# A fused linear-attention and quantised FFN block on one core: reciprocals first on the DMA queue, x by rows two tiles ahead, denominators in front of the products of Q with the state

## What is computed

```python
q, k, v = (norm(x) @ Wq.T + bq), (norm(x) @ Wk.T + bk), (norm(x) @ Wv.T + bv)   # 16 heads of 32
q, k = elu(q) + 1, elu(k) + 1
numerator   = einsum('bhtd,bhtde->bhte', q, cumsum(outer(k, v)))   # causal linear attention
denominator = maximum(einsum('bhtd,bhtd->bht', q, cumsum(k)), 1e-6)
x = x + norm((numerator / denominator) @ Wo.T + bo)
h = mx_quantize(norm(x))              # 32 values share a scale, values on the FP6 grid
x = x + norm(h @ mx_quantize(weight).T + bias)
```

## Time and profile before

| | us |
|---|---|
| median of three runs | 2397.83 |
| lowest and highest | 2393.44, 2398.91 |
| the profiled execution's own time | 2399.21 |
| its span, first to last instruction | 2397.4 |
| mean granted clock of TensorE | 0.993 |

### The profile page before, as it was taken

The page is one execution under the profiler, slowest core; times in us unless marked ns, Lnnn a source line. Parts: engine busy times, 40 slices in busy tenths (PEclk is TensorE's granted clock), DMA queues, the critical chain, the costliest instruction groups (busy, mean ns, idle before and its releaser), DMA issues.

```text
span 2397.4 us, 63827 instructions
## 1 busy us (share of the span) xinstructions
PE 2332.0 (97%) x26146; PEld 1905.0 (79%) x26146; DVE 1984.1 (83%) x3988; ACT 1080.8 (45%) x1840; POOL 1470.3 (61%) x1730
## 2 busy tenths in 40 slices
PE   7999999999999999999999999999999999999997
PEld 5877888888788788888787887888878888878785
DVE  7888889888788888898888887888988888878886
ACT  4444444444444444444444444444444444444442
POOL 2566566666566665666665665656666656656554
PEclk9999999999999999999999999999999999999999
DMA  4222221222222322222322222222123222223211
GB/s 158 71 92 98 75 77 62 88 99 73 86 65 75 99 90 80 77 65 86 99 73 90 73 71 91 96 76 75 62 89 99 73 90 73 71 91 95 77 46 37
DMA packets 108227, 195.55 MB, mean 82 GB/s; under 512 B 15136, under 2 KB 21664, under 8 KB 107424
## 3 DMA queue, kind: packets, MB, share of 16 engines
q1 hardware_dynamic: 107936, 191.47, 24.5%
HBM read 155.65 MB, written 35.78 MB: 80 GB/s over the span
## 4 chain that ended last, share of the span: by engine, by line
PE 79%; DMA 7%; DVE 4%; ACT 3%; issue 3%; POOL 2%; SPq 2%; POOLq 0%; DVEq 0%; ACTq 0%
PE work L423 12%; PE work L425 11%; PE work L424 11%; PE score L423 10%; PE score L424 10%; PE score L425 10%; PE work L540 5%; PE work L442 4%; PE score L505 4%; DMA rden_dram<-rinv 3%; DMA kc<-rden_dram 3%; PE state_bank L553 1%; POOL f_buf L1425 1%; DVE A L1020 1%; PE score L527 1%
## 5 line engine op out<-in xcount | busy, mean ns | idle before, releaser
L1020 DVE TENSOR_TENSOR A<-score,causal 128x512 f32<-128x512 f32 x512 | 329.2, 681 | 21.5 <-PE score L505 21.5
L1395 POOL TENSOR_TENSOR exp_t<-exp_t,x_coef 128x512 f32<-128x512 f32 x124 | 198.5, 1601 | 148.6 <-DMA exp_t<-in_xt 148.6
L725 ACT CAST oT_hi<-kc 128x512 fp32r<-128x512 f32 x128 | 79.6, 622 | 365.4 <-DVE kc L1015 365.4
L1402 POOL TENSOR_TENSOR x_res<-x_res,o_buf 128x512 f32<-128x512 f32 x128 | 175.6, 1372 | 104.5 <-ACT o_buf L670 104.5
L423 PE MATMUL work<-wo_hi,oT_hi 128*128 128x512 f32 x512 | 204.2, 399 | 14.8 <-ACT Kn L720 11.9
L423 PE MATMUL work<-wv_hi,xT_hi 128*128 128x512 f32 x512 | 214.9, 420 | 0.0
L423 PE MATMUL score<-xT_hi,wq_hi 128*128 128x512 f32 x512 | 208.1, 406 | 6.8 <-DVE KT L960 6.8
L1397 POOL TENSOR_TENSOR exp_t<-exp_t,x_coef 128x512 f32<-128x512 f32 x124 | 205.2, 1655 | 9.7
L423 PE MATMUL score<-xT_hi,wk_hi 128*128 128x512 f32 x512 | 205.7, 402 | 0.0
L425 PE MATMUL work<-wv_hi,xT_lo 128*128 128x512 f32 x512 | 202.2, 395 | 0.6 <-issue 0.6
L424 PE MATMUL work<-wv_lo,xT_hi 128*128 128x512 f32 x512 | 201.8, 394 | 0.9 <-issue 0.9
(11 more groups left out here) (134 smaller groups left out, 6393.1 us busy)
## 6 DMA issues: line engine op xcount, KB each, us to landing
x_in<-in_x SPq DMA_DIRECT2D x128, 256.0 KB, 4.3
x_res<-in_x SPq DMA_DIRECT2D x128, 256.0 KB, 2.8
kc<-rden_dram SPq DMA_DIRECT2D x128, 256.0 KB
exp_t<-in_xt SPq DMA_DIRECT2D x124, 256.0 KB, 3.1
out<-f_buf SPq DMA_DIRECT2D x96, 256.0 KB, 2.0
x_coef<-coef_dram SPq DMA_DIRECT2D x31, 512.0 KB, 3.8
out<-xd SPq DMA_DIRECT2D x32, 256.0 KB, 2.1
rden_dram<-rinv SPq DMA_DIRECT2D x32, 64.0 KB, 3.5
```

What stands on the lines that cost most here:

```text
L1020: nc.vector.tensor_tensor(A[:, j, :, :], score_bank[j][:], causal[:].unsqueeze(1).to_broadcast([P, G, P]), ALU.mult).then_inc(a_set, 1)
L1395: nc.gpsimd.tensor_tensor(rows, rows, by_token(0), ALU.mult).then_inc(x_scaled, 1)
L1402: nc.gpsimd.tensor_tensor(x_res[:, b, :], x_res[:, b, :], o_buf[:, b % 2, :], ALU.add).then_inc(r_set, 1)
```

## The change

Four things are moved; no computation is added or taken away.

- SyncE: load_x (x by rows) is issued for tile i+2 instead of i+1, spread over the turn, with tile 1's ahead of the first turn. store_rden comes ahead of the loads of x by features, and these stand between the four spreads. load_res(0) comes behind the third spread, load_res(1), (2) and (3) at the end of the turn, behind store(i-1, 3) and load_x(i+2, 3).
- TensorE: denominators ahead of past_products.
- ScalarE: among others kn(1) ahead of o_hi(0), seed(2) ahead of x_hi(1), xd_hi(1) behind k(3).
- VectorE and GpSimd: the order within the turn is written anew. f_seen(1), its join and its widen stand between phi_q(3) and product(3); x_lo(0) ahead of v_bias(1); o_lo(3) ahead of r_seen(1), as before; x_lo(3) behind quantise(0); output(2) between x_scale(0) and x_scale(1); residual(2) ahead of dequantise(1).

```diff
@@ SyncE, turn @@
-                if nxt:
-                    load_x(i + 1, 0)
-                    load_x(i + 1, 1)
-                    load_x(i + 1, 2)
-                    load_x(i + 1, 3)
+                after = i + 2 < TILES
                 if prev:
                     store(i - 1, 0)
-                if cur:
-                    load_res(i, 0)
+                if after:
+                    load_x(i + 2, 0)
+                    load_x(i + 2, 1)
                 if nxt:
                     store_coef(i + 1)
                     spread_coef(i + 1)
                 if prev:
                     store(i - 1, 1)
-                if cur:
-                    load_res(i, 1)
-                if nxt:
-                    load_xt(i + 1, 0)
-                    load_xt(i + 1, 1)
+                if after:
+                    load_x(i + 2, 2)
                 if cur:
                     store_rden(i)
                     spread_rden(i, 0)
+                if nxt:
+                    load_xt(i + 1, 0)
+                if cur:
                     spread_rden(i, 1)
-                    spread_rden(i, 2)
-                    spread_rden(i, 3)
+                if nxt:
+                    load_xt(i + 1, 1)
                 if prev:
                     store(i - 1, 2)
                 if cur:
-                    load_res(i, 2)
+                    spread_rden(i, 2)
+                    load_res(i, 0)
                 if nxt:
                     load_xt(i + 1, 2)
+                if cur:
+                    spread_rden(i, 3)
+                if nxt:
                     load_xt(i + 1, 3)
                 if prev:
                     store(i - 1, 3)
+                if after:
+                    load_x(i + 2, 3)
                 if cur:
+                    load_res(i, 1)
+                    load_res(i, 2)
                     load_res(i, 3)
@@ TensorE, turn @@
                 f(2)
                 xd_transposes(3)
+                denominators()
                 past_products()
-                denominators()
                 v(0)
@@ ScalarE, turn @@
+                kn(0)
                 seed(0)
-                kn(0)
+                kn(1)
                 o_hi(0)
-                seed(1)
                 if nxt:
                     x_hi(i + 1, 0)
                 f_norm(2)
-                kn(1)
+                seed(1)
+                seed(2)
                 if nxt:
                     x_hi(i + 1, 1)
                 o_hi(1)
                 o_norm(i, 0)
                 kn(2)
-                seed(2)
+                o_hi(2)
+                seed(3)
+                kn(3)
@@ VectorE, turn @@
                 phi_q(0)
+                phi_q(1)
                 xd_lo(2)
-                phi_q(1)
...
-                f_bias(1)
+                phi_q(2)
+                product(2)
+                phi_q(3)
                 f_seen(1)
-                phi_q(2)
...
                 join(i - 1, "f", 1)
-                phi_q(3)
-                product(2)
                 widen(i - 1, "f", 1)
                 product(3)
-                f_bias(2)
                 xd_lo(3)
-                f_seen(2)
                 clamp()
                 invert()
```

More of the change, by code:

```diff
@@ L410, in _ @@
                 load(dst[:], src.to_broadcast([P, D]), small_loaded)
+            for b in range(NSEQ):
+                load_x(1, b)
             turn(0, False, True, True)
@@ L860, in turn @@
                     x_hi(i + 1, 2)
-                o_hi(2)
-                kn(3)
-                seed(3)
                 r_norm(i, 0)
@@ L1251, in turn @@
-                xd_lo(1)
                 join(i - 1, "r", 3)
-                f_seen(0)
-                widen(i - 1, "r", 3)
-                greatest(i - 1, 2)
                 scan(2)
                 join(i - 1, "f", 0)
+                greatest(i - 1, 2)
+                widen(i - 1, "r", 3)
+                scale(i - 1, 2)
                 widen(i - 1, "f", 0)
-                scale(i - 1, 2)
+                xd_lo(1)
                 quantise(i - 1, 2)
+                phi_k(3)
                 if nxt:
-                    widen(i + 1, "x", 2)
+                    join(i + 1, "x", 2)
+                    x_seen(i + 1, 3)
@@ L1263, in turn @@
                 greatest(i - 1, 3)
                 scale(i - 1, 3)
-                phi_k(3)
+                f_bias(1)
                 scan(3)
-                quantise(i - 1, 3)
-                phi_q(0)
-                xd_lo(2)
-                phi_q(1)
                 if nxt:
                     join(i + 1, "x", 3)
-                f_bias(1)
-                f_seen(1)
-                phi_q(2)
+                    widen(i + 1, "x", 2)
+                quantise(i - 1, 3)
                 if nxt:
@@ L1289, in turn @@
+                f_seen(2)
                 v_bias(0)
                 mask(0, 0)
+                join(i - 1, "f", 2)
                 widen(i - 1, "f", 2)
@@ L1296, in turn @@
                 normalise(0)
+                mask(1, 0)
+                f_seen(3)
+                mask(1, 1)
                 o_lo(0)
-                f_seen(3)
-                mask(1, 0)
-                mask(1, 1)
-                join(i - 1, "f", 3)
+                if nxt:
+                    x_lo(i + 1, 0)
                 v_bias(1)
                 mask(1, 2)
+                join(i - 1, "f", 3)
                 mask(1, 3)
+                widen(i - 1, "f", 3)
                 o_bias(i, 0)
-                widen(i - 1, "f", 3)
                 o_seen(i, 0)
-                if nxt:
-                    x_lo(i + 1, 0)
+                normalise(1)
                 join(i, "o", 0)
                 widen(i, "o", 0)
-                normalise(1)
                 mask(2, 0)
@@ L1318, in turn @@
                 mask(2, 2)
+                v_bias(2)
                 mask(2, 3)
-                v_bias(2)
                 r_seen(i, 0)
                 o_bias(i, 1)
+                o_seen(i, 1)
                 join(i, "r", 0)
-                o_seen(i, 1)
+                widen(i, "r", 0)
                 normalise(2)
-                join(i, "o", 1)
                 mask(3, 0)
                 mask(3, 1)
-                widen(i, "r", 0)
+                mask(3, 2)
                 o_lo(2)
-                mask(3, 2)
-                if nxt:
-                    x_lo(i + 1, 2)
+                join(i, "o", 1)
                 mask(3, 3)
+                v_bias(3)
                 widen(i, "o", 1)
-                v_bias(3)
                 greatest(i, 0)
```

70 lines of the change are left out of this document (35 added, 35 removed).

## The result

The changed kernel takes **2472.07 us**, the median of four runs (2460.7 to 2478.17); the kernel before takes 2397.15 (2393.44 to 2398.91) beside it. The ratio is 1.0309, with a 95% interval from 1.0269 to 1.035. The forecast was 2427 and the range ended at 2453: the sign was right, the size was not.

A forecast was written before the change was run, and what follows sets the result against it. TensorE, busy for 97% of the span, was taken to set the time. Kn and masks -21, denominators +27, "issue" -6 and x_res +29 made +29 us; 2399.2 + 29 - 1.4 = 2427 us, range 2385 to 2453.

The forecast's parts named there:

- x_res(1): Its load at the turn's end delays residual(1) through to TensorE's transposes of xd(0): 0.95 us per tile, +29 us (0 to 40).
- The first step of the walk: On GpSimd, residual(1) can't start before 1117.15 instead of 1115.70, waiting for x_res(1) to land: 1.45 us later.
- The 0.35 us that r_seen(1) was to give back: On VectorE, r_seen(1) stands behind o_lo(3), so its join follows at once: about 0.35 us off the x_res(1) wait.
- The slack: Between dequantise(0)'s end at 1120.72 and the transposes of xd(0) at 1121.31: 0.6 us taken off the x_res(1) wait.
- the turn's end: GpSimd's work to output(3) ends later, through seed(2)'s place (+0.15 us) and x_scale(1) (up to +0.7): 0.4 us taken per tile.
- The estimate of 2.6 us for the load: Landing time of x_res(1)'s 256 KB transfer alone, against the row's 3.0 us; would make that term's sum 12 us lower.
- Denominators waiting for product(3): TensorE's denominators, now ahead of the products with the state, wait for VectorE's product(3): 0.87 us per tile, +27 us (16 to 29).
- Kn and masks: TensorE's waits for Kn (11.9 us) and masks (5.6 us) go, with 24 pipeline ends: -21 us (10 to 24).
- "Issue": TensorE's waits without a shown releaser, in the dense stretch, partly absorbed by a pause ahead of it: -6 us (0 to 12).
- Rival (c): x by features loads too late, delaying x_scale(0) and x_lo(0) ahead of the masks: 2442 to 2472, say 2455 us; chance 0.13.

The follow-up runs named there:

- e1: Changed kernel with load_res(1) issued directly behind load_res(0) instead of at the end of the turn; 2449.87 us, 1.0206 of the kernel before.
- e6: Changed kernel with load_res(1) behind load_res(0), product(3) straight behind phi_q(3), and kn(2) ahead of o_norm(0) on ScalarE; 2472.38 us, ratio 1.0302.
- e5: Kernel before with only TensorE's denominators put ahead of the products of Q with the state; 2417.53 us, ratio 1.0073.
- e4: Changed kernel with the 512 KB spread of the norm's factors cut to one partition from tile 2 on, leaving out some computation; 2456.28 us, ratio 1.0237.
- e2: Changed kernel with TensorE's denominators put back behind the products of Q with the state; 2481.73 us, ratio 1.0345.
- e3: Changed kernel with VectorE's product(3) straight behind phi_q(3), ahead of f_seen(1), its join and its widen; 2501.39 us, ratio 1.0427.
- e12: Changed kernel with denominators back behind the products with the state, and x_lo(0) behind mask(1, 3) on VectorE; 2476.23 us, ratio 1.0344.
- e7: e6 with the joins, widens and square roots of the factors of x(2) and x(3) made sooner, so their spread goes out sooner; 2440.95 us, ratio 1.0196.
- e8: Kernel before with only kn(1) moved ahead of o_hi(0) on ScalarE; 2397.09 us, ratio 1.0005.
- e10: Kernel before with kn(1) ahead of o_hi(0), the norm's factors made and spread sooner, and mask(1,0) ahead of o_lo(0) on VectorE; 2371.26 us, ratio 0.9907.
- e11: Kernel before with kn(1) ahead of o_hi(0), factors sooner, mask(1,0) ahead of o_lo(0), and x_res(1) behind the reciprocals' spreads; 2366.64 us, ratio 0.9887.

## Why the prediction was right and wrong

**x_res(1), right.** 0.95 us per tile forecast, 0.94 measured; 29 and 28 us. e1 takes the cause away and wins 22 of it. The first step of the walk was good: with a measured landing time of 3.0 us residual(1) was to start 1.45 us later, and it starts 1.43 later. The rest agrees in the sum by luck. (The forecast's own terms, 0.5 + 0.4, make 0.90 and not 0.95, or 28 us.) The 0.35 us that r_seen(1) was to give back are there, but r_seen(1) itself starts 0.3 us further behind residual(1), since o_lo(3) stands ahead of it; that is new, in the kernel before o_lo(3) stood behind it. The slack gave 0.48 in place of 0.6. And the 0.4 us for the turn's end aren't there: output(3) ends 2.88 us ahead of K(0), in the kernel before 2.53. The estimate of 2.6 us for the load by the Trainium skill (DMA: Bandwidth & Descriptors, "Anatomy of one DMA") would have given 12 us less; the trace sides with the row (median 3.1 for x_res(1), the third of its row of transfers).

**Denominators waiting for product(3), right, and a little small.** 0.87 us forecast, 1.02 measured, 31 us against 27. product(3) ends 0.88 us after TensorE is through with the transposes of xd(3), where 0.81 was forecast (1151.29 - 1150.48); from there to the denominators I took 0.06 us, and the trace shows 0.15. The first turn is left out of both: 3.8 us of waiting in place of 0.6.

**Kn and masks, right where it looked and wrong beyond.** -21 forecast, -19.5 measured at row 0 and A with V. (The first spread goes out 2.7 us sooner after V(0), where I took 1.7, but only 0.4 sooner after K(0): TensorE is later itself.) But the same bank and copy serve row 1 as well, and there 12 waits of up to 0.74 us came up, 0.42 us per tile in the ledger: +13. ScalarE, GpSimd and TensorE at one of them:

```profile
1135.32 0.81 ACT L677 ACTIVATE o_buf<-o_buf,shift_o,rs_o 128x512 f32<-128x512 f32 x1 [1.41 <-POOL shift_o L1385]
1136.04 0.56 ACT L727 COPY Kn<-work 128x512 f32<-128x512 f32 x1
```

```profile
1130.89 1.54 POOL L1400 TENSOR_TENSOR exp_t<-exp_t,x_coef 128x512 f32<-128x512 f32 x1
...
1134.12 1.17 POOL L1385 TENSOR_SCALAR shift_o<-mv_o,rs_o 128x1 f32<-128x1 f32 x1 [0.21 <-POOL rs_o L1382]
```

```profile
1136.66 0.50 PE L430 MATMUL work<-wo_hi,oT_hi 128*128 128x512 f32 x1 [0.74 <-ACT Kn L727]
```

kn(2) stands behind o_norm(0) on ScalarE; o_norm(0) waits for shift_o on GpSimd; and that comes behind x_scale(1), late with its load. That kn(2) is behind o_norm(0) was so before as well. I had carried the lateness of x_scale(1), "up to +0.7 us", to the turn's end and not to this neighbour. e6 puts kn(2) first, and this wait is 0.

**"Issue", wrong in its sign.** Of the terms of the sum this one failed most. -6 forecast; measured 0.72 us before and 1.10 after per tile, +11. I took a pause ahead of the dense stretch for time in which instructions could arrive. But in the trace the packet for this stretch starts only when TensorE is in it, whenever that is, and then takes its turn with the data on the DMA engines. e5 shows the swap alone making these waits longer (12.8 to 17.5 us), e4 shows what of them is the spread. Up to 3 of the 11 us are the clock at 0.5 behind the longest of them, of which the prediction says nothing. What exactly starts a packet wasn't settled, so the part that remains without the spread (about 11 us of the 20) has no shown cause.

**Rival (c), mis-sized, the deepest miss.** I gave x by features too late a chance of 0.13 and wrote it as a sum that is added. That its load would go out "some 3 us later" was right (2.8 us, from V(0)); that x_lo(0) would then be late by 0.6 us at the most was not. It had happened (x_scale(0) 3.7 us later against V(0)), and it isn't added: it takes the place of any other wait ahead of it. In the changed kernel the pause of 1.02 us right ahead of V(0) and the "issue" waits behind it hide most of it, and it shows only as the 13 us at row 1. That the measured time stands at the upper end of (c)'s range is no confirmation of its sum: the masks, where (c) has the wait, are waited for 3.3 us in all. e2, e3, e6 and e12 take that cover away and pay it at the masks, at oT_lo or at Kn. The form "-21 +27 -6 +29" fits the ledger of this kernel, but the 31 us of the denominators couldn't be won back alone; those of x_res(1) (e1) and part of "issue" (e4) could.

From forecast to result, in us: issue 17, row 1 13, first turn 4.7, denominators 4, Kn and masks 1.5, x_res -1, the rest 2.2, which makes 41.4 of 70.6 - 29 = 41.6.

**Open:** the oT_lo and xT_lo waits of e6 and e7, the trigger of an instruction packet, a run with only x by features back ahead of rden's store, and 1.2 us at the end.

## What to carry to other kernels

A queue's order is a budget for all who wait behind it: moving the small urgent store forward meant moving 256 KB loads back. One of them (x_res(1)) stood at the head of a chain of five, and the other (x by features) came to stand behind a transfer that waits for the store's landing. Ask also what the urgent transfer waits for on the queue: here another store, and not its own data. Before an operation that ends a row of waits is moved, ask not only which wait goes but which is the second latest at that place; e8 (wait renamed, gain 0) and e10 (both gone, -26 us for the three steps, -22 by the ratio) are the same edit with and without that question. And where a wait has no releaser, look at which transfers run in the microseconds ahead of it.

## What the hardware showed that I had not expected

TensorE stops for its instructions in the densest stretch, where 128 small products take 1.9 us: every such wait in this stretch of the changed kernel ended 2.2 to 2.8 us after the start of a 16 KB packet. In the six of over 2 us that packet started 2.9 to 3.3 us after the 512 KB spread was issued, in the five others 1.0 to 1.7 us after it. Behind a long one the clock can fall as well: four of the six were followed by 3.4 or 6.8 us at 0.5. At 20.0 us in 11 waits it was the second largest wait of TensorE, for a queue that moves 3.38 MB of 195.55.

A 64 KB store of 32 took between 2.2 and 5.1 us to land in the kernel before, between 2.2 and 4.4 in the changed one; the views of rden_dram in both, in this order:

```profile
DMA to landing us min/median/max: 2.2/3.5/5.1
```

```profile
DMA to landing us min/median/max: 2.2/2.6/4.4
```

So putting the store first did help it, by 0.9 us in the mean (3.61 to 2.73). But x by features now waits for that landing too.

o_lo(0), two operands in SBUF, takes 0.69 us alone and up to 2.12 us beside x_scale (e12; 2.20 in the kernel before). Its mean is 1.20 in the kernel before, 1.25 in e3 and 1.39 in e12, but 0.91 in the changed kernel and 0.82 in e11, where x_scale's passes lie elsewhere. This agrees with the Trainium skill (SBUF — State Buffer, "SBUF: two separate sides"), by which the later one is held until the port pair is free: the o_lo(0) of 2.12 us starts 0.03 us behind an x_scale of 1.60 us and ends 0.55 us after it.
